# Attention norms of batches 0 and 1 placed in graph turns 4 and 15, and the first split of queries and keys placed ahead of the last return to tokens

## The reference, cut to what matters

```
self_feat = concat(v, q) @ W_self.T + b_self            # graph layer
for d in 0, 1:  output += softmax(q_d k_d / 4, masked, + label bias) @ kv @ Wout_d
x = v + relu(output)                                    # what the graph layer hands on, per batch
x1 = layernorm(x) * (scale1 + 1) + shift1               # attention layer
q, k, v = split(x1 @ W_qkv + bias); q, k = l2norm(q) * exp(scale), l2norm(k)
x = x + (softmax(q k) v @ W_proj + b) * gamma1
x = x + gelu-MLP(layernorm(x) * (scale2 + 1) + shift2) * gamma2
```

## Time and profile before

| | before |
|---|---|
| median of 3 runs | 846.36 us (843.59, 846.36, 850.95) |
| the profiled execution | 843.85 us, its span 842.1 us |
| mean granted TensorE clock | 0.969 |
| PE busy | 772.3 us, 92% of the span |
| DVE, ACT, POOL busy | 491.6, 477.2, 380.0 us |
| setup and graph turns 0 and 1, to about 55 us; graph turns on to 249 us | PE 212.8 us busy of the 221 from 28 to 249 |
| seam and attention turn 1, 249 to 301 us | PE 34.6 us busy of 52, clock 0.71 |
| attention, 301 to 619 us | PE 298.1 us busy of 318, clock 0.99 |
| feed-forward, 619 to 842 us | PE 210.9 us busy of 223 |

### The profile page before, as it was taken

One profiled execution on the slowest core, in us unless ns is written; L12 is line 12 of the kernel. 1 busy time (PEld: TensorE's weight loads), 2 busy tenths in 40 slices (PEclk: granted clock), 3 DMA queues, 4 the chain that ended last, 5 costly groups with the idle time before them and its releaser, 6 DMA issues.

```text
span 842.1 us, 15487 instructions
## 1 busy us (share of the span) xinstructions
PE 772.3 (92%) x4964; PEld 566.8 (67%) x4964; DVE 491.6 (58%) x1010; ACT 477.2 (57%) x765; POOL 380.0 (45%) x638
## 2 busy tenths in 40 slices
PE   4989999999988688999999999999868999999997
PEld 3878887878775345666666666666545888888885
DVE  1378888788896545566656666665453344444433
ACT  1334545454434257777777777777746555555553
POOL 0157676666664545555555555554460222222110
PEclk9989999999998679999999999999979999999999
DMA  8701213121200476666666666666720000000001
GB/s 250 238 23 47 93 47 93 49 90 57 82 13 13 80 122 112 109 112 113 115 112 111 112 114 113 111 111 112 119 32 1 1 26 26 26 25 14 26 21 42
DMA packets 68605, 65.59 MB, mean 78 GB/s; under 512 B 10833, under 2 KB 67793, under 8 KB 68561
## 3 DMA queue, kind: packets, MB, share of 16 engines
q1 hardware_dynamic: 67232, 64.87, 36.8%
q10 hardware_dynamic: 1328, 0.16, 0.1%
HBM read 48.09 MB, written 16.78 MB: 77 GB/s over the span
## 4 chain that ended last, share of the span: by engine, by line
PE 66%; ACT 11%; DVE 9%; issue 7%; POOL 1%; DMA 1%; SPq 1%; ACTq 0%; DVEq 0%; POOLq 0%
PE ps L1567 10%; PE ps L1581 10%; PE ps L1293 6%; PE ps L1457 5%; PE ps L1443 5%; ACT probsT L819 4%; PE ps L1495 3%; PE ps L1334 3%; PE ps L1395 3%; PE ps L1269 3%; PE ps L1323 2%; PE ps L1284 2%; PE ps L1387 2%; PE ps L1476 2%; ACT w_ada L848 2%
## 5 line engine op out<-in xcount | busy, mean ns | idle before, releaser
L819 ACT ACTIVATE probsT<-ps 128x1024 f32<-128x1024 f32 x128 | 130.8, 1022 | 49.5 <-PE ps L1443 49.4
L1190 DVE TENSOR_TENSOR hidden_low<-hidden,hidden_high 128x512 fp32r<-128x512 f32 x64 | 46.6, 728 | 107.2 <-ACT hidden_high L930 59.2
L1096 DVE TENSOR_REDUCE neg_max<-ps 128x4 bf16<-128x344 f32 x128 | 64.1, 512 | 56.7 <-PE ps L1410 55.9
L1443 PE MATMUL ps<-q_stack,k_stack 97*128 97x256 bf16 x512 | 79.5, 278 | 10.9 <-ACT probsT L819 6.2
L1443 PEld LDWEIGHTS ps<-q_stack,k_stack 97*128 97x128 bf16 x512 | 43.1, 98 | 67.5 <-issue 30.4
L927 ACT ACTIVATE hidden<-ps,b_fc 128x512 f32<-128x512 f32 x64 | 44.1, 690 | 69.6 <-PE ps L1567 69.6
L1457 PE MATMUL ps<-probsT,v_ones 128*32 128x256 f32 x1024 | 68.5, 385 | 9.1 <-ACT probsT L819 9.0
L606 POOL TENSOR_TENSOR scores<-scores,row_max 128x640 f32<-128x640 f32 x32 | 40.7, 1271 | 78.6 <-DVE row_max L965 78.6
L1387 PE MATMUL ps<-w_qkv,x1T 128*128 128x512 f32 x128 | 66.3, 643 | 1.5 <-DVE rest L1103 1.5
L1293 PE MATMUL ps<-x_res,w_q 128*128 (+1 forms) x256 | 63.0, 390 | 0.0
L1293 PEld LDWEIGHTS ps<-x_res,w_q 128*128 128x128 f32 x256 | 46.8, 192 | 10.9 <-issue 5.5
(11 more groups left out here) (173 smaller groups left out, 1903.7 us busy)
## 6 DMA issues: line engine op xcount, KB each, us to landing
parts_dram<-w_ada SPq DMA_DIRECT2D x96, 128.0 KB
q_stack<-parts_dram SPq DMA_DIRECT2D x96, 128.0 KB, 4.5
adj<-in_adj SPq DMA_DIRECT2D x16, 440.0 KB, 4.3
k_stack<-parts_dram SPq DMA_DIRECT2D x16, 384.0 KB, 7.9
xT<-in_xT SPq DMA_DIRECT2D x16, 256.0 KB, 2.9
x_in<-in_x SPq DMA_DIRECT2D x16, 256.0 KB, 2.7
k_stack<-parts_dram SPq DMA_DIRECT2D x16, 256.0 KB, 8.7
out_x<-result SPq DMA_DIRECT2D x16, 256.0 KB, 2.1
```

The lines of the kernel that those rows point to most:

```text
L819: nc.scalar.activation(probsT[:, s % 4, :], ps[:, COLS:COLS + 2, :].rearrange("p a n -> p (a n)"), ACT.Exp).then_inc(exp_made, 1)
L1096: nc.vector.tensor_reduce(places[:, :, k], ps[:, ROW_BANKS[n % 2], 0:4 * KP].rearrange("p (a g) -> p a g", a=4), AX_X, ALU.max, negate=Tru ...
L1190: nc.vector.tensor_tensor(hidden_parts[1][:, s % H_SLOTS, :], hidden[:, s % RAW, :], hidden_parts[0][:, s % H_SLOTS, :], ALU.subtract).the ...
L1443: mm = nc.tensor.matmul(ps[:, COLS + j, kt * N:(kt + 1) * N], k_stack[:, par, place, kt * P:(kt + 1) * P], q_stack[:, par, place, :], star ...
```

## The change

Moments, root and normalisation of batch 0 are issued in graph turn 4; moments and root of batch 1 in graph turn 15, its normalisation in the seam. In the seam DVE no longer does `moments(1)`, and `normalise(1)` stands ahead of `take_qk(0, 0)` instead of behind `first_guess(0)`. POOL's memset goes behind `low_part(0, 0, 1)`. On PE `norm_transposed(1)` precedes `graph_tokens(B - 2)`, and `split_qk(0)` precedes `graph_tokens(B - 1)`. No instruction is added or removed in total.

```diff
+    MOMENTS_AT = (4, B - 1)
 # POOL, graph_turn, behind v_masked and ahead of POOL's two normalise
-            if isinstance(f, int) and f == B - 1:
-                norm_root(pool, nc, 0, mean_var, g, var_eps, rstd, mv_made, eps_made, rstd_made)
+            if isinstance(f, int) and f in MOMENTS_AT:
+                norm_root(pool, nc, MOMENTS_AT.index(f), mean_var, g, var_eps, rstd, mv_made, eps_made, rstd_made)
 # POOL, seam
         shift(B - 1, 1, 0)
-        norm_root(pool, nc, 1, mean_var, g, var_eps, rstd, mv_made, eps_made, rstd_made)
         shift(B - 1, 1, 1)
         normalise(B - 1, 1, 0)
         normalise(B - 1, 1, 1)
         roots(0)
         pool.wait_ge(x_made, B)
-        nc.gpsimd.memset(v_ones[:, :, :, :, HD:2 * HD], 1.0).then_inc(ones_set, 1)
         blocks_of_pairs(0, 0)
         low_part(0, 0, 0)
         low_part(0, 0, 1)
+        nc.gpsimd.memset(v_ones[:, :, :, :, HD:2 * HD], 1.0).then_inc(ones_set, 1)
 # DVE, graph_turn
             if b is not None:
                 graph_scores(b, 1 - par, 1)
-            if isinstance(f, int) and f == B - 1:
-                moments(0)
+            if isinstance(f, int) and f in MOMENTS_AT:
+                moments(MOMENTS_AT.index(f))
             if c is not None:
                 take_output(c)
...
             if f is not None:
                 edge_biases(f, par)
-            if isinstance(f, int) and f == B - 1:
-                normalise(0)
             if c is not None:
                 graph_residual(c, par)
+            if isinstance(f, int) and f == MOMENTS_AT[0]:
+                normalise(0)
 # DVE, seam
         graph_scores(B - 1, 1, 0)
-        moments(1)
         graph_scores(B - 1, 1, 1)
+        normalise(1)
         take_qk(0, 0)
         sums(B - 1, 1, 0)
         take_qk(0, 1)
...
         first_guess(0)
-        normalise(1)
         take_output(B - 2)
         graph_residual(B - 2, 0)
+        dve.wait_ge(g["late_weights"], g["LATE"])
         unit_qk(0)
         take_output(B - 1)
         graph_residual(B - 1, 1)
         dve.wait_ge(x_made, B)
-        dve.wait_ge(g["late_weights"], g["LATE"])
 # PE, seam
         weights_of(B - 1, 1, 0)
-        graph_tokens(B - 2, B)
         pe.wait_ge(aff_out, 2 * T * B)
         norm_transposed(1)
+        graph_tokens(B - 2, B)
         weights_of(B - 1, 1, 1)
         graph_channels(B - 1, 1, B)
+        split_qk(0, None)
         graph_tokens(B - 1, B)
-        split_qk(0, None)
```

## The result

The changed kernel takes 838.94 us (median of 15 runs, 834.69 to 841.95) against 843.59 us for the kernel before (15 runs, 840.53 to 850.95). The ratio is 0.9934, 95% interval 0.9917 to 0.9951: 5.6 us less, 4.1 to 7.0. Beside other kernels on the chip the same changed kernel later gave 0.9945 (0.9925 to 0.9964) and 0.9947 (0.9924 to 0.9970). It is one of the faster ones, 2.0 us under the median of its kernel, while that of the kernel before lies 0.3 us above its own; so 6.9 us is more than the clocked times bear out.

A forecast was written before the change was run, and what follows sets the result against it. PE bounds graph turns and attention, with waits in the seam between. Seam gain 7.2 less 1.5 us in turn 4 saves 5.7 us: 846.36 to 840.7 us; own case 838.4 to 842.4, all cases 835.5 to 847.5.

The forecast's parts named there:

- the term for it: Seam: POOL's sums of keys start 8.1 to 6.4 us earlier; 7.2 us taken as the gain.
- Norm of batch 0 out of the way: Seam: second raw scores 2.9 us earlier, then full clock; second `make_qk` at 255.4 instead of 259.87.
- Normalisation of batch 1 ahead: Seam, DVE: takes 0.73 us, or 1.76 if POOL holds it; free, or 0.3 us if held.
- Roots, split: Seam: unit queries and keys at 268.1, 4.4 us earlier; split starts at 268.2 instead of 276.21.
- Last residual and sums: End of seam: last residual at 270.6 to 272.3, POOL's sums at 270.7 to 272.4 instead of 278.83.
- Memset: POOL, seam: its 0.95 us move out of the way, though hidden before behind the wait for the high parts.
- Turn 4: Graph turn 4: normalisation held by POOL, `nonzero` at 99.1, PE loses 1.5 us; bounds 0.7 and 2.0 us.
- the 1.8 us worked out from the rule: Turn 4's cost if the exclusive lock alone decides, DVE ending about 0.7 us after POOL.
- The clock didn't fall in turn 5: Rivals with a turn 5 clock fall: 844.9 us with half-clock seam end (0.22), or slower, 847.6 us (0.07).
- The gain wasn't hidden: Rival: first column scores bound by something not moved, only turn 4's cost stays; 847.9 us, chance 0.05.
- More than forecast: Rival: 0.7 us lost in turn 4, full-clock seam (8.1) and attention turn 1; 9.3 us saved, 837.1 us, chance 0.14.
- 6.6 us: Saving if the clock falls only after an idle stretch: 8.1 us in the seam less 1.5 in turn 4.

The follow-up runs named there:

- e8: Changed kernel with batch 0's norm in DVE's waits, batch 1's statistics and root likewise in turn 15, low parts first, gated bias behind the rests; 836.73 us, ratio 0.9911.
- e7b: Changed kernel with four extra 128x512 adds on DVE ahead of batch 0's normalisation in graph turn 4; 845.46 us, ratio 1.0025 to the kernel before.
- e1: Changed kernel with the first split of queries and keys behind the last return to tokens again; ratio 0.9960 to the kernel before.
- e4: Changed kernel with batch 1's normalisation behind the first guess of the roots again; ratio 0.9945 to the kernel before.
- e0: The changed kernel run again without any edit; ratio 0.9945 to the kernel before.
- e5: Changed kernel with POOL's two low parts of batch 0 ahead of its two key-block multiplications; ratio 0.9933 to the kernel before.
- e6: Changed kernel with POOL's memset ahead of the sums of keys again; ratio 0.9941 to the kernel before.
- e10: The changed kernel once more, as neighbour to the second run of the version with all four moves; 838.01 us, ratio 0.9947 to the kernel before.
- e2: Changed kernel with the norms of batches 0 and 1 placed as in the kernel before, other reordering kept; ratio 0.9967 to the kernel before.
- e3: Changed kernel with batch 0's statistics and normalisation in DVE's waits of turns 3 and 4, root in POOL's turn 3; 839.71 us, ratio 0.9947.
- e9: The version with all four moves run once more, beside the changed kernel; 835.63 us, ratio 0.9905 to the kernel before.

## Why the prediction was right

Forecast was 840.7 us, 5.7 us under a median of 846.36; measured are 5.6 us by the ratio, and 838.94 us, because the kernel before has a median of 843.59 over more runs. That the saving came out to a tenth is in part luck, for two errors offset each other. The seam gave 1.1 us more than the term for it. And the prediction let all time won ahead of attention turn 2 reach the end. The traces of the changed kernel have the column scores 7.0 to 7.2 us earlier than before, but the clocked times differ by 5.6, 4.6 and 4.5 us, and the last two intervals (3.0 to 6.3 and 2.5 to 6.4) leave 7 us out. Some 1.4 to 2.8 us are thus not found again at the end. With one trace of the kernel before, no run shows where they went.

- *Norm of batch 0 out of the way.* Right. Second raw scores 252.59, predicted 251.05 plus the 1.5 us of turn 5; second `make_qk` 256.82, predicted 255.4 plus 1.5. Full clock there, as taken.
- *Normalisation of batch 1 ahead.* Right in both halves: held to 1.68 us, and covered by the wait for the second `make_qk` but for 0.3 us at the second add of queries (0.3 was predicted for the held case). The experiment that put it back showed a benefit that I had not counted, a PE that isn't kept waiting.
- *Roots, split.* Unit queries at 269.65, predicted 268.1 plus 1.5; split at 269.70.
- *Last residual and sums.* 270.6 to 272.3 was predicted, 7.2 us taken for the gain. Measured without the slip: 6.79 + 1.51 = 8.3 us. This is the term that was mis-sized, by 1.1 us: I had allowed for half clock at the end of the seam, and the three gaps of 1.75, 1.11 and 1.00 us left the clock full in all three traces of the changed kernel. At full clock the prediction had the last residual at 270.6; it ends at 271.96 - 1.51 = 270.45. In e8 and e7b, whose gaps there are the same to 0.03 us, the split was at half clock, so the allowance is not unfounded; in e1 and e4, with another order, it fell as well.
- *Memset.* That it was hidden before is as predicted; the prediction's "out of the way" understated it, since its move is worth 0.9 us in the new order.
- *Turn 4.* Right to a tenth: 1.51 us for 1.5, `nonzero` at 99.04 for 99.1, by the step described: held by POOL, then `cond`, raw scores and weights late. Undoing it moved everything up to the sums forward by 1.5 us; making the stay longer moved it back, by 3.8 us in turn 5 and 4.2 us at turn 15 and the split.
- The Trainium skill (SBUF — State Buffer, SBUF: two separate sides) has the lock held for the whole instruction by whoever is first. The trace agrees in turn 4 that DVE is held: a normalisation issued at 97.97, while POOL worked until 98.65, took 1.15 us. It doesn't agree in size: it ended 0.47 us after POOL and not the 0.73 us that it takes alone, and the 1.8 us worked out from the rule are 0.3 too many.
- *Rivals.* The clock didn't fall in turn 5 in any of the traces with the changed turn 4 (changed, e0, e1, e4, e5, e6, e10 show 15.37 or 15.38 us). The gain wasn't hidden. "More than forecast" was near for the seam, but turn 5 took its full price and `make_qk` of attention turn 1 took 3.34 us, not the 1.88 of full clock.

By the Trainium skill (TensorE: Matmul & The Clock Gate, What's actually happening) neither turn 5 nor the seam's gaps would lower the clock, which gave 6.6 us. Turn 5 and the seam of the changed kernel agree with it in all three traces, and the sums came 6.8 us earlier. Other runs don't: in e8 the clock fell in a seam whose gaps were 1.74, 1.11 and 0.99 us, in e4 behind one of 1.96 us.

## What to carry to other kernels

A small step moved out of a crowded place isn't free in the place that takes it: look there for the idle time of its own engine (here 1.2 us between the nonzero test and the features) and for the other engine that may hold it. In a stage that one engine bounds, a microsecond inserted ahead of its inputs was kept here through all the turns that followed. What was hidden behind a wait must be looked at again once that wait is gone, as the memset here; and shortening a chain pays only up to the next one, as the low parts by themselves did in their one trace.

## What the runs showed that I had not expected

- The scatter between executions of one kernel lies at both ends of the traces, not between them. Three executions of the changed kernel agree within 0.1 us from turn 5 to POOL's sums and within 0.23 us up to the column scores. The start of turn 5 lies at 94.10 to 98.02 us in the thirteen traces. From the column scores to the end it is 540.9 to 541.4 us in the four traces with a clock of 1.00 between 588 and 612 us (before, changed, e1, e2), 542.9 to 543.6 us in the six with 0.92 or 0.93, and 545.1 or 545.2 us in the three with 0.86 (e0, e3, e10). That the clock is the cause is not shown; the two go together.
- Nearly the same gaps of 1.0 to 1.8 us in the seam were followed by a split of 1.09 us at full clock in some executions and of 1.78 to 1.97 us in others; with all moves together this happened between two executions of one kernel (e8 and e9).
